# Gate steps to GpSimd, three layer norms to ScalarE, and a new order of steps in a four-stage transformer kernel

## The reference, cut to what matters

```python
def _layernorm(x, axis=-1, eps=1e-05):
    m = jnp.mean(x, axis=axis, keepdims=True)
    v = jnp.var(x, axis=axis, keepdims=True)
    return (x - m) / jnp.sqrt(v + eps)
...
# L0 mixer: per head of 16, fft of q and kv, both normalised, kv summed along the rows
qf = _l2_normalize_complex(jnp.fft.fft(q, axis=-1))
kvf = jnp.cumsum(_l2_normalize_complex(jnp.fft.fft(kv, axis=-1)), axis=1)
values = jnp.fft.ifft(qf * kvf, axis=-1).real.reshape(B, S, D) @ W_o.T
...
# L0 feed-forward: eight gates, the best one picks a low-rank expert
cont = jnp.einsum('nds,bntd->bnts', select_weight, x_diff) ** 2
score = cont.sum(axis=-1)
gate = jax.nn.sigmoid(imp_slope[None, :, None] * (score - imp_center[None, :, None]))
sel_scale = gate.max(axis=1)[..., None]
sel_idx = gate.argmax(axis=1)
...
return (1.0 - sel_scale) * x + sel_scale * mod_x_bias
...
# L1 mixer: softmax attention, 16 heads of 16; L1 feed-forward:
h = jnp.square(jax.nn.relu(jnp.einsum('bsd,hd->bsh', x, w1)))
return jnp.einsum('bsh,dh->bsd', _rms_norm(h), w2)
...
x = _layernorm(x + _L0_attn_ref(...)); x = _layernorm(x + _L0_ffn_ref(...))
x = _layernorm(x + _L1_attn_ref(...)); x = _layernorm(x + _L1_ffn_ref(...))
```

## Time and profile before

| | before |
|---|---|
| median of 3 runs | 784.78 us (781.06 to 786.9) |
| the profiled execution's own time | 784.01 us |
| its span | 782.0 us |
| PE busy | 671.8 us, 86% |
| DVE busy | 587.1 us, 75% |
| ACT busy | 474.3 us, 61% |
| POOL busy | 346.7 us, 44% |
| mean granted TensorE clock | 0.951 |

### The profile page before, as it was taken

One profiled execution on the slowest core, in us unless ns is written; L12 is line 12 of the kernel. 1 busy time (PEld: TensorE's weight loads), 2 busy tenths in 40 slices (PEclk: granted clock), 3 DMA queues, 4 the chain that ended last, 5 costly groups with the idle time before them and its releaser, 6 DMA issues.

```text
span 782.0 us, 15196 instructions
## 1 busy us (share of the span) xinstructions
PE 671.8 (86%) x5316; PEld 531.2 (68%) x5316; DVE 587.1 (75%) x1416; ACT 474.3 (61%) x958; POOL 346.7 (44%) x537
## 2 busy tenths in 40 slices
PE   4556657798998999999989999989999988989894
PEld 3334545476876878787868787878787776766684
DVE  4795548697979898989898888978787976647131
ACT  4323133648676676767585858585858584955931
POOL 4302302114447373727272727282647352735555
PEclk9578688999999999999999999999999999999998
DMA  7200053627162616171626352635343534371000
GB/s 206 67 1 14 14 86 77 126 52 138 27 135 41 137 39 135 35 137 38 118 60 103 75 87 64 106 100 85 92 82 83 79 86 77 87 129 37 15 14 14
DMA packets 298171, 60.59 MB, mean 77 GB/s; under 512 B 237352, under 2 KB 293616, under 8 KB 298096
## 3 DMA queue, kind: packets, MB, share of 16 engines
q1 hardware_dynamic: 298096, 59.63, 37.7%
HBM read 38.38 MB, written 20.97 MB: 76 GB/s over the span
## 4 chain that ended last, share of the span: by engine, by line
PE 33%; DVE 28%; SPq 16%; DMA 8%; issue 5%; ACT 5%; POOL 4%; POOLq 0%; ACTq 0%; DVEq 0%
SPq L754 13%; DVE nmax L1623 9%; PE pB L974 5%; PE pA L958 4%; DMA kT<-qk_scratch 4%; PE pO L1026 3%; PE pC L1075 3%; DMA qk_scratch<-qk_part 3%; PE pA L869 3%; PE pC L1097 2%; PE pA L851 2%; PE pS L1000 2%; PE pA L904 2%; DVE spec L1465 2%; PE pS L1050 1%
## 5 line engine op out<-in xcount | busy, mean ns | idle before, releaser
L1623 DVE TENSOR_REDUCE nmax<-pB 128x2 f32<-128x512 f32 x256 | 166.0, 680 | 35.3 <-PE pB L974 34.7
L1246 ACT ACTIVATE pt<-pS 128x512 f32<-128x512 f32 x256 | 147.8, 605 | 61.9 <-PE pS L1000 61.5
L974 PE MATMUL pB<-kT,qT 96*128 96x256 bf16 x512 | 90.8, 279 | 25.4 <-DVE nmax L1623 15.8
L1793 POOL TENSOR_TENSOR hsum<-hsum,hsq 128x512 f32<-128x512 f32 x48 | 64.8, 1349 | 56.3 <-ACT hsq L1286 56.3
L1000 PE MATMUL pS<-qT,kT 98*128 98x256 bf16 x512 | 86.2, 275 | 3.6 <-ACT pt L1246 2.5
L1816 POOL TENSOR_TENSOR hid_lo<-hh,hid 128x512 fp32r<-128x512 f32 x64 | 83.9, 1310 | 4.5 <-ACT hh L1296 4.0
L974 PEld LDWEIGHTS pB<-kT,qT 96*128 96x128 bf16 x512 | 38.8, 99 | 58.8 <-DVE nmax L1623 38.1
L1075 PE MATMUL pC<-x3T,w1T 128*128 128x256 f32 x256 | 68.2, 301 | 4.7 <-ACT hr L1274 4.2
L1026 PE MATMUL pO<-pt,v_ext 128*32 128x256 f32 x1024 | 68.9, 387 | 3.1 <-ACT pt L1246 2.9
L1738 POOL TENSOR_SCALAR vea<-mva 128x2 f32<-128x2 f32 x16 | 3.6, 223 | 148.7 <-DVE mva L1422 148.5
L1097 PE MATMUL pC<-w2T,hid 128*128 128x256 f32 x256 | 63.0, 288 | 0.0
(11 more groups left out here) (178 smaller groups left out, 1783.5 us busy)
## 6 DMA issues: line engine op xcount, KB each, us to landing
qk_scratch<-qk_part SPq DMA_DIRECT2D x48, 256.0 KB, 4.8
qT<-qk_scratch SPq DMA_DIRECT2D x96, 128.0 KB, 2.9
kT<-qk_scratch SPq DMA_DIRECT2D x96, 128.0 KB, 2.7
xa<-in_x SPq DMA_DIRECT2D x16, 256.0 KB, 3.0
v_scratch<-qkv SPq DMA_DIRECT2D x16, 256.0 KB, 3.8
v_heads<-v_scratch SPq DMA_DIRECT2D x16, 256.0 KB, 2.8
out_y<-y SPq DMA_DIRECT2D x16, 256.0 KB, 2.0
pt<-in_wfc SPq DMA_DIRECT2D x1, 1024.0 KB, 7.5
```

The lines of the kernel that those rows point to most:

```text
L974: ins = pe.matmul(pB[h % 2][:, s * T:(s + 1) * T], qT[k][0:STACK, u * P:(u + 1) * P], kT[k][0:STACK, h * T:(h + 1) * T], start=True, stop= ...
L1246: act.activation(pt[:, (h // 4) % 2, h % 4].rearrange("p s n -> p (s n)"), pS[h % 2][:], ACT.Exp, scale=HD ** -0.5).then_inc(S["probs"], 1)
L1623: dve.tensor_reduce(nmax[:, h * SIDES:(h + 1) * SIDES], pB[h % 2][:].rearrange("p (s k) -> p s k", s=SIDES), AX.X, ALU.max, negate=True).t ...
L1793: pool.tensor_tensor(hsum[:], hsum[:], hsq[:], ALU.add).then_inc(S["hsum_done"], 1)
```

## The change

It moves work and rewrites all three lists.

- To POOL: eight of the gate's instructions, as `g_terms` (2), `g_score` (3) and `g_pick` (3). What stays on DVE is `g_gate1_0`, one reduction and one reciprocal (`g_gate1_1`), and `g_gate2_0` to `_5`. The semaphore `gate_step` is replaced by ten smaller ones.
- To ACT: `a_norm1`, `g_norm2` and `e_norm`, as an activation with scale and bias. The bias is minus mean times inverse root, so each of the three POOL steps `a_pow1`, `g_pow2` and `e_pow` makes two more small instructions.
- To DVE: for batches 13 to 15 (`LATE = 13`) the low parts (`c_vlo` in place of `c_lo`) and the last norm (`c_vnorm` in place of `c_norm`).
- `ORDER`, `FILL` and `DRAIN` are new on all engines. Turns are counted from another step (`b_max_0` on PE), so most shifts differ by one without the step having moved. PE runs the same matmuls, except that `p_stir` has other counts.

```diff
+LATE = 13
...
-    "b_max_13:+2 b_max_14:+2 e_outt_0:+2 b_max_15:+2 e_outt_1:+2 a_proj_1 c_ms:+2 b_maxt_t:+2 e_ont:+2 "
+    "b_max_0:+1 b_max_1:+1 e_out_2:+1 b_max_2:+1 a_xt:-1 e_score_13:+1 b_max_3:+1 c_hid_2:+1 b_max_4:+1 "
...
+            def norm(r, rs, nb, done):
+                for s in range(SIDES):
+                    act.activation(r[:, s, :], r[:, s, :], ACT.Identity, bias=nb[:, s:s + 1], scale=rs[:, s:s + 1]
+                                   ).then_inc(done, 1)
+
+            def a_norm1(i, k):
+                act.wait_ge(S["a_pow"], nth(i, PER["a_pow"], 1))
+                norm(x1[k], rsa, nba, S["x1_done"])
...
-            def norm(r, mv, rs, done):
-                for s in range(SIDES):
-                    dve.tensor_scalar(r[:, s, :], r[:, s, :], mv[:, s, 0:1], rs[:, s:s + 1],
-                                      ALU.subtract, ALU.mult).then_inc(done, 1)
...
-                elif n == 1:
-                    dve.wait_ge(S["gate_read"], nth(i, PER["gate_read"], 1))
-                    dve.wait_ge(S["x1_sq"], nth(i, PER["x1_sq"], 2))
-                    dve.tensor_tensor(f2[:], f[:, :, 0:G_M], f[:, :, 0:G_M], ALU.mult).then_inc(S["gate_step"], 1)
-                    dve.tensor_tensor(gt[:, 1], f[:, :, G_M:G_U], each(s2[:]), ALU.add).then_inc(S["gate_step"], 1)
...
+            def c_vlo(i, g):
+                if i < LATE:
+                    return
...
+                dve.tensor_tensor(hid_lo[:, 2 * g:2 * g + 2].rearrange("p c n -> p (c n)"), hh[:, g % 2, :],
+                                  hid[:, 2 * g:2 * g + 2].rearrange("p c n -> p (c n)").bitcast(F32),
+                                  ALU.subtract).then_inc(S["lo_done"], 1)
...
+                pool.tensor_scalar(nma[:].rearrange("p (s a) -> p s a", a=1), mva[:, :, 0:1], -1.0, None, ALU.mult
+                                   ).then_inc(S["a_eps"], 1)
                 plus_eps(vea, mva, S["a_eps"])
-                pool.wait_ge(S["a_eps"], nth(i, PER["a_eps"], 1))
-                root(rsa, vea, S["a_pow"])
+                pool.wait_ge(S["a_eps"], nth(i, PER["a_eps"], 2))
+                root(rsa, vea, S["a_rs"])
+                pool.wait_ge(S["a_rs"], nth(i, PER["a_rs"], 1))
+                pool.tensor_tensor(nba[:], nma[:], rsa[:], ALU.mult).then_inc(S["a_pow"], 1)
...
+            def g_terms(i, k):
+                pool.wait_ge(S["gate_read"], nth(i, PER["gate_read"], 1))
+                pool.wait_ge(S["x1_sq"], nth(i, PER["x1_sq"], 2))
+                pool.tensor_tensor(f2[:], f[:, :, 0:G_M], f[:, :, 0:G_M], ALU.mult).then_inc(S["gate_terms"], 1)
+                pool.tensor_tensor(gt[:, 1], f[:, :, G_M:G_U], each(s2[:]), ALU.add).then_inc(S["gate_terms"], 1)
+
+            def g_score(i, k):
+                pool.wait_ge(S["gate_ratio"], nth(i, PER["gate_ratio"], 2))
+                pool.tensor_tensor(gt[:, 3], gt[:, 0], gt[:, 2], ALU.mult).then_inc(S["gate_score"], 1)
...
+            def g_pick(i, k):
+                pool.wait_ge(S["gate_sel"], nth(i, PER["gate_sel"], 1))
+                pool.tensor_scalar(two_less[:], sel, -1.0, 2.0, ALU.mult, ALU.add).then_inc(S["gate_rest"], 1)
+                pool.wait_ge(S["gate_one"], nth(i, PER["gate_one"], 1))
+                pool.tensor_tensor(mix[:, :, EXPERTS * RANK:MIX], gt[:, 10], each(sel), ALU.mult
+                                   ).then_inc(S["gate_pick"], 1)
```

167 lines of the change are left out of this document (98 added, 69 removed), and 619 rows, old and new, of tables (DRAIN, FILL, ORDER).

## The result

| | before | changed |
|---|---|---|
| median | 782.0 us (12 runs, 778.79 to 786.9) | 778.26 us (12 runs, 777.29 to 780.22) |
| profiled execution, its span | 784.01, 782.0 us | 780.22, 778.3 us |
| PE, DVE, ACT, POOL busy | 671.8, 587.1, 474.3, 346.7 us | 677.7, 525.7, 517.8, 382.5 us |
| mean granted clock | 0.951 | 0.944 |

The ratio is 0.9934, with a 95% interval of 0.9913 to 0.9954: faster by 0.7%, within 1% of no change. The forecast was 761.5 us, with a range from 749 to 778; the median lies 0.3 us above the range. The work moved as it was meant to; the time did not follow.

A forecast was written before the change was run, and what follows sets the result against it. PE was taken as nearly full but not setting the turn alone, waiting on DVE's row maxima. Ten turns -12.0, three turns -3.0, start -3.5, 632 to 715 us -1.0, end -3.0: 784.0 - 22.5 = 761.5 us, range 749 to 778.

The forecast's parts named there:

- what moves where: Busy time per turn: DVE loses 6.2 us, POOL gains 3.8, ACT gains 2.7.
- the end: Last batches: low part and last norm leave POOL's chain for DVE, with gains for batches 13 and 14; -3.0 us.
- the steady turn: One full turn in the middle falls to 39.2 us, 1.2 less, with 38.2 and 40.4 as ends.
- Idle ACT of 11.9 us covers it: Per turn, ACT's idle time was to absorb the six norm activations, priced at 0.45 us each, 2.7 in all.
- The loop through ACT: From c_hid_2 through PE, DVE, POOL and ACT to the second c_relu: 38.7 us a turn.
- the sum over ten turns: Fourth to fourteenth batch: ten full turns at -1.2 us each, -12.0 us.
- the start and the turns behind it: Stretch up to the fourth batch's b_max_0: -3.5 us before the first b_max_0, -3.0 in the turns after it.
- the three turns: Turns before the ten full ones, with DVE busy for 91 of 109 us: -1.0 us each, -3.0.
- from 632 to 715 us: From the fourteenth batch's b_max_0 to the last b_max: the gate is over soon, -1.0 us.
- ACT's: Rival: norms wait in ACT's queue for POOL, the middle gains nothing, only start and end do; 777.5 us, chance 0.17.
- The exclusion: Rival: POOL's added SBUF reads and DVE's two-input steps block each other, 1.3 us lost in each of 13 turns; 768, chance 0.16.
- PE's floor: Rival: PE's waits and some slow starts go, the turn falls to 38.2 us; 750 us in all, chance 0.17.

The follow-up runs named there:

- x_norm_dve: Changed kernel with the three norms back on DVE, without the bias instructions on POOL; ratio to the kernel before 0.9872, steady turn 39.22 us.
- v_low_later: w_store_later with g_low also moved behind c_bn on DVE; ratio to the kernel before 0.9942, steady turn 39.53 us.
- x_order_only: Changed kernel's new order and lists with norms, gate and last batches' work on the engines of before; ratio to the kernel before 1.0167.
- z_gate_alone: Kernel before, in its own order, with only the gate's eight instructions moved to POOL; ratio to the kernel before 1.0192.
- w_store_later: Changed kernel with c_norm behind g_pow2 on POOL and c_store behind g_v_in on SP; ratio to the kernel before 0.9947, steady turn 39.53 us.
- x_tail_pool: Changed kernel with LATE = 16: low parts and last norm of batches 13 to 15 back on POOL; ratio to the kernel before 0.9993.

## Why the prediction was wrong, point by point

The forecast difference was 22.5 us, the one between the two profiles is 3.7. Of the 18.8 us between them 9.6 lie in the start and the three turns behind it, 6.7 in the ten turns, 2.1 in the turns behind those, and 0.4 at the end.

**Right: what moves where.** DVE -6.2 a turn (measured 5.9), POOL +3.8 (4.1), ACT +2.7 (2.9), the score at 0.25 us on POOL (0.22 for two of three), the wait for row maxima under 0.5 us a turn (0.43).

**Near by luck: the end, -3.0 forecast, -2.6 measured.** Its last `c_y` (L1113) took 5.58 us:

```profile
766.12 5.58 PE pC L1113 x32
...
775.08 0.41 DVE y L1701
```

```profile
766.00:772.00 6.00, 5.68 (x34) 5.37 (x32) 0.28 (x2) 0.00 (x0) 0.70 (x1) 0.72 0.00 0
```

The granted clock was 0.72 from 766 to 772 us; with 1.00 the same 32 matmuls took 4.05 us in the kernel before. Of the twelve kernels with this end and all matmuls six have 5.6 us there and six 4.1. Where it is 4.1 and the norms are on ACT, the end takes 63.1 us, 4.1 less than before. So the work that left POOL's chain gave more than forecast, and the clock took 1.5 us of it back in this profile.

**Wrong: the steady turn, -1.2 forecast, -0.6 measured.** The step that failed is "Idle ACT of 11.9 us covers it", and with it the price of the norm on ACT. The text took 0.45 us from a square of the same size and kept 0.6 as the bound; it is 0.59, and with the overlap of the two sides the six cost 3.3 us a turn, 0.6 more than the 2.7 counted. The Trainium skill (ScalarE: Activation LUTs, "What ACT_TABLE_LOAD costs") gives 186 ns + 0.833 ns a column for an activation and about 93 ns more for each operand of one value per partition. By that the norm, which has two, comes to 585 ns as an estimate; the rows have 589 to 593, and agree. The loop through ACT was named and came to 38.7; the 0.6 alone makes it 39.3. I took 39.2 as if the loops ended side by side and then hid the norms in ACT's 9 idle us. Here idle time of an engine that works in order covered nothing for the step that was next in its queue: x_norm_dve puts the loss at 0.61 us. That this kernel, with the norms on DVE, turns in the 39.2 that was forecast with them on ACT is chance. `c_norm` ahead of `a_pow1`, worth 0.3 us, was not in the forecast's loops.

**Wrong: the sum over ten turns, -12.0 forecast, -5.3 measured.** Beside the turn's size this holds a slip of 3 us: two starts 40.40 apart stood for all turns, but 401 us are 40.1 a turn, and ten turns of 39.2 would have saved 9. Nor do the norms explain the other 3.7: with them on DVE the ten turns still took 394.1 to 395.1 us where nothing else held them up. The four steady turns stood for ten, of which five come from lists written out step by step and run from 36 to 43 us. The wait for row maxima, read as 1.5 us a turn from four turns, is 11.8 us in all ten.

**Wrong: the start and the turns behind it, -6.5 forecast, +3.1 measured.** For the start (-3.5 forecast) the step that failed is the carrying of the gain at `a_even` to the end of the stretch. The 4.1 us came and were gone 28 us later, at the second batch's `a_even`: a norm and squares on ACT, POOL held up beside weight steps, PE on the lower clock. The first `b_max_0` scatters from 121.3 to 123.5 us against 122.0 before, so the +1.5 is no loss that one profile can show. For the three turns (-3.0 forecast) DVE's 91 busy us of 109 were taken for a wait. PE waited only 1.4 us for row maxima there in the kernel before; in the changed one it waits 2.1 us for norms on ACT, and the three turns take 110.0 to 111.7 us in the ten kernels with this list, the norms on ACT, the gate on POOL and whole row maxima, against 109.1. Two experiments on the start moved single steps and neither gave the time back.

**Wrong: from 632 to 715 us, -1.0 forecast, +1.1 measured.** With the norms on DVE it is -2.7 (80.0 us), so here too the norms on ACT are the term that was put at nothing.

**The rivals.** ACT's, at 777.5 and with 0.17, came nearest in time. Its reason, ACT's queue, is the one that the runs bear out for half of the turn's gain; that the middle gives nothing is not, and it kept the full 6.5 us of start and end, of which the start's 3.5 did not come. The exclusion did move with the work: 0.8 us on `nmb`, 0.4 on the third score instruction, 1.9 twice in the start, and 0.9 on `g_gate2_0` on DVE. v_low_later shows that the first cost nothing in the turn; the last is on the chain, and no run took it away. The Trainium skill (SBUF — State Buffer, "Who interferes with whom") has it that a DVE instruction with two SBUF inputs contends with a POOL instruction that reads SBUF, and the trace agrees: `nmb` falls from 1.00 to 0.24 when no such DVE instruction starts ahead of it. PE's floor was not reached, and PE is not the bound for being busy for 96% of a turn either: 1.5 us less of its work changed nothing.

**What the prediction lacked** is the view of the order as a part of the change with a price of its own. It costed the moves and let the lists follow; x_order_only and z_gate_alone show that each without the other loses 1.7 to 1.9% (the latter in the order of before, fitted by hand to the old split).

## What to carry to other kernels

Moving work off a busy engine paid here where that engine's instructions stood between two that another engine waits for, and only with an order that had the receiving engine free at that moment: a gain together, a loss of 1.7 to 1.9% apart. Before work goes to an engine that is idle a third of the time, follow the chain through its queue and price the new instruction there, with the operands it will have. When a busy engine is suspected as the bound, take some of its work away: if the turn stays the same, look for the loop, in the very kernel that you will edit; and when a step is moved in a test, look at every queue that waits for its result, the one that issues transfers among them. A gain early in a start is worth nothing until it is followed to the step that ends the stretch.

## What the runs showed of the hardware

An activation of 128x256 with scale and bias from SBUF took 0.59 us, two in a row 1.09, a square of the same size 0.42 to 0.45. A POOL instruction of 0.23 to 0.29 us took 1.0 us beside a DVE instruction of 1.19 with two SBUF inputs and 2.2 beside one of 2.4. Of the score instructions of 128x16 the first two took 0.22 us on POOL and the third 0.64; on DVE, in a kernel whose POOL was in 1.3 us instructions, the first two took 0.85 and 1.22. A DVE instruction of 128x16 with one input took 0.12 us in most turns of the kernel before and 0.98 in the changed one, beside such an instruction of POOL. The clock late in the run differed between profiles of the same steps: the last 32 matmuls took 5.6 us at a mean granted clock of 0.72 in the changed kernel, 4.05 at 1.00 in the kernel before and in w_store_later, and 6.0 at 0.51 in x_tail_pool.
